# Moving the four weight sums of a unit from GpSimd to VectorE in a Strassen-style attention kernel

## What is computed

```python
W = weights[condition]                       # one of 16 matrices 64x64 for each of 64 samples
y = einsum('bct,bcd->bdt', x, W)             # x is 64 x 64 x 1024
qkv = y @ attn_qkvw + attn_qkvb              # 1024 -> 3072
q, k, v = heads(qkv)                         # 32 heads of 32, sequence 64
probs = softmax(q k^T / sqrt(32))
x = x + (probs v) @ attn_ow + attn_ob
x = x + ffn(expert_linear(x))                # top-2 expert LoRA linear, quantised SwiGLU
```

## Time and profile before

| | us |
|---|---|
| three runs, median (lowest to highest) | 2159.0 (2158.58 to 2160.08) |
| the profiled execution, whole | 2156.13 |
| its span | 2154.5 |
| TensorE busy | 2083.1 (97%) |
| VectorE busy | 1418.4 (66%) |
| GpSimd busy | 1394.3 (65%) |
| ScalarE busy | 1045.9 (49%) |

### The profile page before, as it was taken

The page is one execution under the profiler, slowest core; times in us unless marked ns, Lnnn a source line. Parts: engine busy times, 40 slices in busy tenths (PEclk is TensorE's granted clock), DMA queues, the critical chain, the costliest instruction groups (busy, mean ns, idle before and its releaser), DMA issues.

```text
span 2154.5 us, 45958 instructions
## 1 busy us (share of the span) xinstructions
PE 2083.1 (97%) x18120; PEld 1697.2 (79%) x18120; DVE 1418.4 (66%) x2395; ACT 1045.9 (49%) x1364; POOL 1394.3 (65%) x1138
## 2 busy tenths in 40 slices
PE   6999999999999999999998899999999999999996
PEld 5888878888778888788887788887777787787784
DVE  6355565565565554655557855656788888888987
ACT  4356665565565566656655321223444344344343
POOL 6888888888889888889886700001455555555553
PEclk8999999999999999999999999999999999999998
DMA  3255644554644555455557255468344344434433
GB/s 123 61 125 112 126 138 116 110 130 101 153 110 112 116 111 120 130 116 112 125 112 235 98 196 176 152 188 243 76 112 109 97 105 112 105 95 117 107 78 98
DMA packets 413165, 267.05 MB, mean 124 GB/s; under 512 B 275778, under 2 KB 344514, under 8 KB 412482
## 3 DMA queue, kind: packets, MB, share of 16 engines
q1 hardware_dynamic: 410130, 261.38, 47.3%
q0 software_dynamic: 2864, 3.28, 0.9%
HBM read 152.92 MB, written 50.33 MB: 94 GB/s over the span
## 4 chain that ended last, share of the span: by engine, by line
PE 82%; POOL 7%; DVE 4%; DMA 3%; issue 2%; ACT 1%; SPq 1%; POOLq 0%; DVEq 0%; ACTq 0%
PE acc L811 36%; PE acc L1757 16%; PE acc L1225 6%; PE att L1225 6%; PE att L1784 5%; POOL w_slot_lo L401 3%; PE att L1727 3%; PE att L840 3%; PE acc L1793 2%; POOL w_raw L404 2%; PE acc L1766 2%; PE att L867 2%; POOL w_slot_hi L399 2%; DMA w_raw<-wu 2%; DMA x_raw<-x 1%
## 5 line engine op out<-in xcount | busy, mean ns | idle before, releaser
L811 PE MATMUL acc<-y_hi,w_slot_hi 128*128 128x512 f32 x1344 | 533.9, 397 | 12.8 <-issue 7.2
L811 PE MATMUL acc<-y_lo,w_slot_hi 128*128 128x512 f32 x1344 | 526.6, 392 | 0.0
L811 PE MATMUL acc<-y_hi,w_slot_lo 128*128 128x512 f32 x1344 | 525.8, 391 | 0.0
L401 POOL TENSOR_TENSOR w_slot_lo<-w_raw,w_slot_hi 128x512 fp32r<-128x512 f32 x329 | 432.3, 1314 | 26.3
L811 PEld LDWEIGHTS acc<-y_hi,w_slot_hi 128*128 128x128 f32 x1344 | 254.1, 189 | 70.1 <-issue 13.5
L404 POOL TENSOR_TENSOR w_raw<-w_raw 128x512 f32<-128x512 f32 x188 | 251.7, 1339 | 75.8 <-DMA w_raw<-wu 68.6
L811 PEld LDWEIGHTS acc<-y_hi,w_slot_lo 128*128 128x128 f32 x1344 | 254.1, 189 | 54.0
L811 PEld LDWEIGHTS acc<-y_lo,w_slot_hi 128*128 128x128 f32 x1344 | 254.3, 189 | 50.5
L632 DVE TENSOR_REDUCE top<-att 128x8 f32<-128x512 f32 x126 | 86.4, 686 | 250.7 <-PE att L840 248.4
L663 DVE TENSOR_TENSOR unit<-acc,unit 128x512 f32<-128x512 f32 x144 | 99.4, 690 | 212.7 <-PE acc L811 212.4
L399 POOL CAST w_slot_hi<-w_raw 128x512 fp32r<-128x512 f32 x329 | 222.9, 677 | 12.3 <-PE acc L811 0.2
(11 more groups left out here) (184 smaller groups left out, 3969.6 us busy)
## 6 DMA issues: line engine op xcount, KB each, us to landing
w_raw<-wu SPq DMA_DIRECT2D x192, 256.0 KB, 3.2
c_raw<-context_T SPq DMA_DIRECT2D x16, 1024.0 KB, 6.2
f_x_all<-x_T SPq DMA_DIRECT2D x32, 512.0 KB, 4.8
f_xr_all<-x_T SPq DMA_DIRECT2D x32, 512.0 KB, 6.1
out<-f_raw SPq DMA_DIRECT2D x31, 512.0 KB, 3.4
context_T<-cx SPq DMA_DIRECT2D x60, 256.0 KB, 3.3
x_raw<-x SPq DMA_DIRECT2D x27, 512.0 KB, 4.4
xa<-xT SPq DMA_DIRECT2D x12, 1024.0 KB, 7.0
```

Source lines behind the costliest of these rows:

```text
L401: pool.tensor_tensor(w_lo[:, k], raw, w_hi[:, k].bitcast(F32), ALU.subtract).then_inc(w_set, 1)
L811: ins = pe.matmul(bank, w[:, k, c, :], v[:, k, c, :], start=(k in (0, 1, 5) and c == 0 and i == 0), stop=(c == C // 2 - 1 and i == 2), ski ...
```

## The change

The four sums of unit U+1 are made by VectorE (`mix`, now in its stream) at the end of steps 1 to 4 of unit U. In the first unit of each later block (units 12, 24 and 36), where R22 of the next unit arrives late, they come at steps 4, 4, 5 and 6. GpSimd keeps the splits and waits for the sums by `w_mix`. The registers in which the sums lie are renamed so that split 1 to 4 read R21, R11, R21, R11; therefore SP now reloads R21 before R11 (after splits 3 and 4). Sum i waits for sum i-1 and for split i-1 (`w_set`), sum 0 for R21 and R22 to have landed, sum 2 for R12. Unit 0's own sums are VectorE's in both kernels, so 4 x 47 = 188 sums move.

```diff
-                sp.wait_ge(w_set, SLOTS * (U - 2) + (4, 6, 5, 7)[reg])
+                sp.wait_ge(w_set, SLOTS * (U - 2) + (5, 6, 4, 7)[reg])
...
                     if k == 4:
+                        load_w(U + 2, R21)
+                    elif k == 5:
                         load_w(U + 2, R11)
-                    elif k == 5:
-                        load_w(U + 2, R21)
...
         def refill_w(U, k):
             if k == 0:
                 pool.wait_ge(w_in[R11], 16 * (U + 1))
-                split(U, 0, R11)
...
+            elif k < 5:
+                pool.wait_ge(w_mix, 4 * (U - 1) + k)
+            elif k == 6:
                 pool.wait_ge(w_in[R22], 16 * (U + 1))
...
+            split(U, k, (R11, R21, R11, R21, R11, R12, R22)[k])
...
+        def summed(U, k):
+
+            if U and U % UNITS == 0:
+                return {4: (0, 1), 5: (2,), 6: (3,)}.get(k, ())
+            return (k - 1,) if 0 < k < 5 else ()
+
+        def mix(U, i):
+
+            dst, a, b, op = ((R21, R21, R22, ALU.add), (R11, R21, R11, ALU.subtract),
+                             (R21, R12, R11, ALU.subtract), (R11, R22, R11, ALU.subtract))[i]
+            if i == 0:
+                dve.wait_ge(w_in[R21], 16 * (U + 1))
+                dve.wait_ge(w_in[R22], 16 * (U + 1))
+            else:
+                dve.wait_ge(w_mix, 4 * (U - 1) + i)
+                dve.wait_ge(w_set, SLOTS * (U - 1) + i)
+            if i == 2:
+                dve.wait_ge(w_in[R12], 16 * (U + 1))
+            dve.tensor_tensor(w_raw[:, dst], w_raw[:, a], w_raw[:, b], op).then_inc(w_mix, 1)
...
+                if U + 1 < ALL:
+                    for i in summed(U, k):
+                        mix(U + 1, i)
```

More of the change, by code:

```diff
@@ L401, in split @@
             pool.tensor_tensor(w_lo[:, k], raw, w_hi[:, k].bitcast(F32), ALU.subtract).then_inc(w_set, 1)
-        def mix(U, i, dst, a, b, op):
-            pool.tensor_tensor(w_raw[:, dst], w_raw[:, a], w_raw[:, b], op).then_inc(w_mix, 1)
-            pool.wait_ge(w_mix, 4 * U + i - 3)
         def refill_w(U, k):
@@ L409, in refill_w @@
                 pool.wait_ge(w_in[R11], 16 * (U + 1))
-                split(U, 0, R11)
-            elif k == 1:
-                pool.wait_ge(w_in[R21], 16 * (U + 1))
+            elif k < 5:
+                pool.wait_ge(w_mix, 4 * (U - 1) + k)
+            elif k == 6:
                 pool.wait_ge(w_in[R22], 16 * (U + 1))
[L414 to L429, removed]
+            split(U, k, (R11, R21, R11, R21, R11, R12, R22)[k])
         def low(k, p):
```

## The result

| | before | after |
|---|---|---|
| median of 6 runs each, us (lowest to highest) | 2158.8 (2153.85 to 2161.24) | 2178.5 (2176.15 to 2180.0) |
| the profiled execution, whole / its span | 2156.13 / 2154.5 | 2178.22 / 2176.4 |
| VectorE busy, GpSimd busy | 1418.4, 1394.3 | 1552.2, 1163.0 |

The changed kernel takes 1.009 of the time of the one before (95% interval 1.0073 to 1.0106), 19.7 us more. GpSimd works 231 us less, VectorE 134 more, and the program is slower.

What follows compares the result with a forecast made beforehand. TensorE was taken to bound the units, so relieving GpSimd gains nothing. 2156.1 + 12.0 (R22 stalls) + 0.3 (first units) + 5.1 (half clock) - 0.7 (block end) = 2172.8; with 2.9 to the median, about 2176 us, range 2161 to 2184.

Runs made afterwards that it cites:

- experiments 3 and 7: 3: the changed kernel with R22 loaded ahead of R12, 2170.0 us; 7: the changed kernel with plain copies in place of SyncE's transposing DMAs, 2172.4 us.

## What to carry to other kernels

An operation that waits for a DMA must not stand in an in-order stream ahead of one that the bottleneck waits for; put it right behind, and if several units share the code, compare the landing with the engine's arrival in each kind of unit, not only in the odd one. When such a wait appears in the profile of the old kernel under another engine, it moves with the work: its landing time against the new engine's arrival is the price. One profile shows one execution; a lead that looks ample there may be thin in the next, and relieving an engine that nobody seems to wait for can still be worth a few microseconds.

## What the runs showed of the hardware

- The 256 KB load of R22 in the changed kernel took 2.9 to 3.6 us from issue to landing in units with no transposing DMA near it, 4.0 to 6.1 us between two of them, and 3.6 to 4.1 us there when those were plain copies of the same bytes; the load of R12 just ahead of it then took 3.6 to 5.8 us. At the same size the place in the queue counted: issued first of the pair, R22 was under way 3.7 us in unit 10 instead of 6.1.
- VectorE's multiplication by a constant (128x512, fp32, in place) took 0.43 us at its shortest and 1.44 to 1.48 just behind a subtraction that GpSimd had begun; with two operands 0.69 and 1.73. Making the operation 0.26 us shorter made the turn only 0.27 shorter, of 1.73.
- The granted clock behind an idle TensorE of 2.5 or 2.6 us at the same place of the program was 0.50 in one execution and 1.00 in another. The starts of unit 24 before (row first) and after:

```profile
604.63 0.77 PE L811 MATMUL acc<-y_hi,w_slot_hi 128*128 128x512 f32 x1 [2.64 <-issue]
```

```profile
616.18 0.47 PE L815 MATMUL acc<-y_hi,w_slot_hi 128*128 128x512 f32 x1 [2.50 <-issue]
```

Behind stalls with 3.5 us of idle and more it was 0.50 each time (nine of nine in the changed kernel and experiments 3 and 7). In units 2 to 47 of all fourteen profiles, idle stretches of 1.3 to 1.9 us were followed by it in none of 56 cases, those of 1.9 to 2.8 us in 22 of 46, longer ones in 13 of 13. What decides between 1.9 and 2.8 us was not tried.
